# A GELU network's first product: y and its weights in two scaled fp16 parts each, three products of parts in place of float32 ones

## What is computed

```python
def _L1_attn_ref(x, wq, wk, wv, w1, b1, w2, b2, g1, be1, g2, be2):   # D_MODEL = 256, D_FF = 1024
    ...                                    # linear attention: msg
    x = x + msg
    x2 = _layernorm(x, g2, be2)            # the kernel's y
    h = jax.nn.gelu(x2 @ w1.T + b1, approximate=False)
    x = x + (h @ w2.T + b2)
    return x
...
x = L0_attn_inputs
x = x + _layernorm(_L0_attn_ref(_layernorm(x), ...))
x = x + _layernorm(_L0_ffn_ref(_layernorm(x), ...))
x = x + _layernorm(_L1_attn_ref(_layernorm(x), ...))
x = x + _layernorm(_L1_ffn_ref(_layernorm(x), ...))
```

## Time and profile before

| | |
|---|---|
| Timed executions | 3266.88, 3273.56, 3274.42 us, median 3273.56 |
| Profiled execution | 3264.48 us, of which 3262.7 us is the span from its first to its last instruction |
| Mean granted TensorE clock | 0.979 of 2.4 GHz |
| Softmax attention | from 0 to about 2047 us |
| Later layers | from about 2047 us to the end |
| Busy in the span | TensorE matmul 90%, ScalarE 71%, VectorE 46%, GpSimd 7% |
| Memory traffic | 54 GB/s on average |

### The profile page before, as it was taken

How to read it: one execution, slowest core, us unless ns; L and a number is a source line. 1 busy time by engine, 2 the same in 40 slices (tenths; PEclk the granted TensorE clock), 3 DMA queues, 4 the chain that set the end, 5 groups by cost and what they waited for, 6 DMA issues and landing times. The chain is left out here.

```text
span 3262.7 us, 47962 instructions
## 1 busy us (share of the span) xinstructions
PE 2933.2 (90%) x18048; PEld 1175.9 (36%) x18048; DVE 1487.4 (46%) x3540; ACT 2324.9 (71%) x2581; POOL 217.2 (7%) x193
## 2 busy tenths in 40 slices
PE   0899998999999999999999999389999999999986
PEld 0121221222222222222222222156666666666654
DVE  7231130322432333223420311558888888866674
ACT  0999999999999999999999999223333333433332
POOL 0000000000000000000000000011111111111110
PEclk9999999999999999999999999689999999999998
DMA  3310110310210221111110110212111211111010
GB/s 121 117 51 27 54 54 25 92 53 25 80 54 24 80 80 34 50 54 50 61 53 25 48 35 26 66 46 79 57 59 58 81 60 58 45 46 59 26 46 21
DMA packets 124714, 177.69 MB, mean 54 GB/s; under 512 B 41936, under 2 KB 99536, under 8 KB 124240
## 3 DMA queue, kind: packets, MB, share of 16 engines
q1 hardware_dynamic: 124496, 174.76, 16.6%
HBM read 107.62 MB, written 67.11 MB: 54 GB/s over the span
## 5 line engine op out<-in xcount | busy, mean ns | idle before, releaser
L663 ACT ACTIVATE probs<-ps 128x1024 f32<-128x1024 f32 x2048 | 1894.8, 1172 | 49.2 <-PE ps L436 48.0
L562 PE MATMUL ps<-probs,vals 128*32 128x512 f32 x8192 | 1097.8, 609 | 0.0
L436 PE MATMUL ps<-qT,kT 64*128 64x512 f16 x4096 | 731.2, 387 | 109.9 <-DMA kT<-split_dram 27.9
L436 PEld LDWEIGHTS ps<-qT,kT 64*128 64x128 f16 x4096 | 173.7, 93 | 1151.2 <-ACT probs L663 1026.6
L811 DVE COPY sums<-ps 128x512 f32<-128x512 f32 x64 | 44.3, 692 | 527.6 <-PE ps L562 527.6
L562 PEld LDWEIGHTS ps<-probs,vals 128*32 128x32 f32 x8192 | 163.0, 108 | 297.6 <-issue 234.0
L1235 PE MATMUL layers_ps<-yT,weight_mem 128*128 128x512 f32 x512 | 227.5, 595 | 10.9 <-ACT hT L1474 10.9
L1241 PE MATMUL layers_ps<-weight_mem,hT 128*128 128x256 f32 x1024 | 231.5, 380 | 0.0
L1501 ACT ACTIVATE gate<-layers_ps 128x512 f32<-128x512 f32 x96 | 57.3, 597 | 224.4 <-PE layers_ps L1389 224.4
L1241 PEld LDWEIGHTS layers_ps<-weight_mem,hT 128*128 128x128 f32 x1024 | 193.5, 190 | 29.4
L1389 PE MATMUL layers_ps<-n4T,weight_mem 128*128 128x512 f16 x768 | 177.0, 385 | 7.3 <-DVE n4T L1724 7.3
(11 more groups left out here) (223 smaller groups left out, 2614.9 us busy)
## 6 DMA issues: line engine op xcount, KB each, us to landing
split_dram<-parts SPq DMA_DIRECT2D x28, 768.0 KB, 3.7
qT<-split_dram SPq DMA_DIRECT2D x128, 128.0 KB
kT<-split_dram SPq DMA_DIRECT2D x128, 128.0 KB
xs<-in_x_dram SPq DMA_DIRECT2D x4, 2048.0 KB, 13.2
qT<-split_dram SPq DMA_DIRECT2D x128, 64.0 KB
kT<-split_dram SPq DMA_DIRECT2D x128, 64.0 KB
heads_dram<-result SPq DMA_DIRECT2D x64, 128.0 KB, 7.5
q_in<-q_dram SPq DMA_DIRECT2D x16, 512.0 KB, 3.3
```

The costliest lines, as they stand in the source:

```text
L436: last = nc.tensor.matmul(SCORES[slot][:, n * BANK:(n + 1) * BANK], kT[buf][rows, j * P:(j + 1) * P], qT[buf][rows, q0:q0 + BANK], start=T ...
L562: mm = nc.tensor.matmul(ACC[32 * c:32 * c + 32, :], vals[buf][:, j, :], probs[:, j % PROBS, c * BANK:(c + 1) * BANK], start=(j == 0), stop ...
L663: nc.scalar.activation(probs[:, j % PROBS, half * T // 2:(half + 1) * T // 2], SCORES[slot_of(at)], ACT.Exp, scale=OPERAND_SCALE ** -2).th ...
```

## The change

The float32 products of `fc0` and `fc1` are replaced by fp16 ones. y and `w1` are each multiplied by a scale and split into a high and a low fp16 part. For each block of 128 hidden channels TensorE makes three products of parts (high w1 with high y, low w1 with high y, high w1 with low y), each over two halves of the 256 channels: six fp16 matmuls of 512 columns in place of two float32 ones. GELU gets the inverse scale as a per-partition operand.

ScalarE now writes the high part (with the scale) and raises `yT_high`; a new VectorE stage `y_low` makes the low part from PSUM and raises `yT_done`. `y_low` stands behind `k_feat` in the list of `all` and between `o` and `diag` in that of `drain`. In the softmax program VectorE finds the largest `w1` at head 57, makes the scales at head 58 (nine small instructions) and splits `w1` in place at head 59 (three instructions over 2048 columns).

```diff
-STAGES = {... "m": "msg y yT",
+STAGES = {... "m": "msg y yT y_low",
...
-    "all": "ffn x4 b2 mix out n4 in0 n4_low f up0 up1 low0 low1 x2 up2 up3 low2 low3 msg n2 up4 up5 low4 low5 u y k_low o k_feat in1 q_low in2 q_feat kv diag".split(),
-    "drain": "x4 b2 ffn n4 out n4_low up0 up1 low0 low1 up2 up3 low2 low3 msg up4 up5 low4 low5 y o diag".split()}
+    "all": "ffn x4 b2 mix out n4 in0 n4_low f up0 up1 low0 low1 x2 up2 up3 low2 low3 msg n2 up4 up5 low4 low5 u y k_low o k_feat y_low in1 q_low in2 q_feat kv diag".split(),
+    "drain": "x4 b2 ffn n4 out n4_low up0 up1 low0 low1 up2 up3 low2 low3 msg up4 up5 low4 low5 y o y_low diag".split()}
...
@@ TensorE, fc
-                        chan_out(ps[:, 6 + i % 2, :], W["w1"], i, yT).then_inc(sem("fc_mm"), 1)
+                        for n, (s, t) in enumerate(((0, 0), (1, 0), (0, 1))):
+                            for k in range(KC):
+                                last = nc.tensor.matmul(ps[:, 6 + i % 2, :], w1_16[:, s, k, i * P:(i + 1) * P], yT16[:, t, k, :],
+                                                        start=(n == k == 0), stop=(n == 2 and k == KC - 1))
+                        last.then_inc(sem("fc_mm"), 1)
@@ ScalarE
-                A(yT[:, :, :], banks(0, 2), ACT.Copy).then_inc(sem("yT_done"), 1)
+                A(yT16[:, 0, :, :], banks(0, 2), ACT.Copy, scale=y_scale).then_inc(sem("yT_high"), 1)
...
-                        A(hT[:, i, :], ps[:, 6 + i % 2, :], ACT.Gelu, bias=W["b1"][:, 0, i:i + 1]).then_inc(sem("gelu_done"), 1)
+                        A(hT[:, i, :], ps[:, 6 + i % 2, :], ACT.Gelu, scale=fc_back, bias=W["b1"][:, 0, i:i + 1]).then_inc(sem("gelu_done"), 1)
@@ VectorE
+            def y_low(c, past):
+                dve.wait_ge(sem("yT_high"), c + 1)
+                V.scalar_tensor_tensor(yT16[:, 1, :, :].rearrange("p a n -> p (a n)"), wide(0, 2), y_scale, yT16[:, 0, :, :].rearrange("p a n -> p (a n)"),
+                                       ALU.mult, ALU.subtract).then_inc(sem("yT_done"), 1)
@@ VectorE, softmax program, heads 57 to 59
+                    V.tensor_reduce(widest_weight[:, 1:2], flat(W["w1"]), AX.X, ALU.max, apply_absolute_value=True).then_inc(weights_ready, 1)
...
+            def parts_of_w1():
+                ...
+                ch.link(V.tensor_scalar(scaled, w1, fc_scale[:, 1:2], None, ALU.mult))
+                ch.link(V.tensor_copy(high, scaled))
+                ch.link(V.tensor_tensor(low, scaled, high, ALU.subtract))
```

More of the change, by code:

```diff
@@ L68 @@
 NORM_SCALE, HIDDEN_SCALE = 2048.0, 0.5
+W1_MAX, Y_MAX = 2.0 ** 12, 2.0 ** 14
+ROOT_C = C ** 0.5
 FLOAT_WEIGHTS = (("wr", KC, C), ("wk", KC, C), ("wv", KC, C), ("aq", KC, C), ("akv", KC, 2 * C), ("w1", KC, F1), ("w2", M1, C),
@@ new lines, in first_half, with scales_of_w1 @@
+                    scales_of_w1()
+                if last_group and e == 3:
+                    parts_of_w1()
+            def scales_of_w1():
+                ch = Chain(dve, weights_ready, 3)
+                tmp = lambda i: fc_scale[:, i:i + 1]
+                ch.done(V.tensor_scalar(tmp(4), widest_weight[:, 3:4], TINY, None, ALU.max))
+                ch.done(V.tensor_reduce(tmp(5), W["g2"], AX.X, ALU.max, apply_absolute_value=True))
+                ch.link(V.tensor_reduce(tmp(6), W["be2"], AX.X, ALU.max, apply_absolute_value=True))
+                ch.link(V.scalar_tensor_tensor(tmp(3), tmp(5), ROOT_C, tmp(6), ALU.mult, ALU.add))
+                ch.link(V.tensor_scalar(tmp(3), tmp(3), TINY, None, ALU.max))
+                ch.link(V.reciprocal(fc_scale[:, 0:2], fc_scale[:, 3:5]))
+                ch.done(V.tensor_scalar(tmp(0), tmp(0), Y_MAX, None, ALU.mult))
+                ch.done(V.tensor_scalar(tmp(1), tmp(1), W1_MAX, None, ALU.mult))
+                ch.link(V.scalar_tensor_tensor(tmp(2), tmp(3), 1 / (Y_MAX * W1_MAX), tmp(4), ALU.mult, ALU.mult))
+                assert ch.n == W1_SCALED - 3
@@ L985, in second_half @@
+            def parts_of_w1():
+                ch = Chain(dve, weights_ready, W1_SCALED)
+                scaled, w1 = flat(xs[:, 0:KC * F1 // C, :]), flat(W["w1"])
+                high, low = (w1.bitcast(FP16)[:, s * KC * F1:(s + 1) * KC * F1] for s in range(2))
+                ch.link(V.tensor_scalar(scaled, w1, fc_scale[:, 1:2], None, ALU.mult))
+                ch.link(V.tensor_copy(high, scaled))
+                ch.link(V.tensor_tensor(low, scaled, high, ALU.subtract))
             def second_half(head, general):
@@ L1022, in _ @@
             second_half(NHD - 1, False)
-            dve.wait_ge(weights_ready, 3)
+            dve.wait_ge(weights_ready, W1_SCALED + 3)
 SHIFT = {"0": -EARLY, "1": 1 - EARLY, "2": 2 - EARLY, "l": LEAD, "m": LEAD + 1, "a": LEAD + 2, "b": LEAD + 3, "c": LEAD + 4}
 FIRST_CHUNK = {stream: EARLY if stream in "012" else 0 for stream in SHIFT}
-STAGES = {"0": "load_in in0 in1 in2 keep_x1", "1": "mix mix_r mix_k val f x2 n2 u", "2": "uT k k_low k_feat v q q_low q_feat kv", "l": "load_msg diag", "m": "msg y yT",
+STAGES = {"0": "load_in in0 in1 in2 keep_x1", "1": "mix mix_r mix_k val f x2 n2 u", "2": "uT k k_low k_feat v q q_low q_feat kv", "l": "load_msg diag", "m": "msg y yT y_low",
           "a": "load_x2 b2 fc0 fc1 proj0 proj1 proj2 proj3 o",
@@ L1100, in run, with later_layers @@
                 once(it, first, streams)
-def later_layers(nc, heads_in, x_in, W, W16, int_weights, narrow, ident, x2_dram, n2_dram, q_dram, kv_sums, sem, out):
+def later_layers(nc, heads_in, x_in, W, W16, int_weights, narrow, ident, x2_dram, n2_dram, q_dram, kv_sums, fc_scale, sem, out):
     with ExitStack() as ctx:
@@ L1761, in program @@
                 stages = {"in0": in0, "in1": in1, "in2": in2, "mix": mix, "f": f_layer, "x2": x2_layer, "n2": n2_layer, "u": u_layer,
-                          "k_low": k_low, "k_feat": k_features, "q_low": q_low, "q_feat": q_features, "kv": kv, "diag": diag, "msg": msg, "y": y_in,
+                          "k_low": k_low, "k_feat": k_features, "q_low": q_low, "q_feat": q_features, "kv": kv, "diag": diag, "msg": msg, "y": y_in, "y_low": y_low,
                           "o": o_layer, "x4": x4_layer, "n4": n4_layer, "ffn": ffn_stats(exact16), "out": finish,
```

19 lines of the change are left out of this document (12 added, 7 removed).

## The result

The changed kernel takes 3300.05 us (median of four, 3298.27 to 3300.99); the kernel before, run beside it, 3273.99 (3266.88 to 3274.49). The ratio is 1.0079, with a 95% interval of 1.0067 to 1.0092: 26 us slower. The profiled execution took 3300.85 us, with a span of 3299.0 us and a mean granted clock of 0.966, where before had 3262.7 and 0.979.

A forecast was written before the change was run, and what follows sets the result against it. Bound: TensorE from `mix_k` to `k`, then VectorE from `k_low` to `mix`. Order +5.1 and clock +15.5 make +20.6 us on 3264.48, giving 3285; taken as 3290 towards the timed median, range 3268 to 3307.

The forecast's parts named there:

- the order: VectorE's chain in iterations 5 to 12: `y_low`, taken as 1.23 us, is paid eight times, +9.8 us.
- The products: `fc` blocks on TensorE: 0.43 us less a block, 55 us for 128 blocks, bringing nothing in iterations 5 to 12.
- The rival that TensorE counts: Waits before `mix_k` come from TensorE's own lateness, so 55 us less work shows in full: 3210 us; chance 8%.
- The clock at `mix_k`: Waits of 4.6 us before every `mix_k` lower TensorE's clock: +9.5 us (bounds 0 and +13).
- The wait before `q`: TensorE waits 2.3 us for `yT_done`; clock lost in about half the cases, +6 including drain waits (bounds 0 and +9).
- Iterations 12 to 14: `q` comes 2.3 to 2.6 us later with nothing queued on VectorE to cover it: +3.1 us of order.
- The drain: Iterations 15 to 18: TensorE's savings against `y_low` give -7.8 us of order; clock at waits before `up0` costs +2.
- Softmax program: Preparing `w1` on VectorE at three heads falls into its idle time: 0 us (bounds 0 and +5).
- The partial rival: VectorE's slow `xk` loses its collision, 2 us in 8 iterations, with little clock loss: -10 to -30; chance 4%.
- the rival with an unchanged clock: Order costs +5.1 us, `mix_k` slows no more often than now: 3270 (3279 against the median); chance 22%.

The follow-up runs named there:

- `y_low` alone: The kernel before with float32 products kept and only a VectorE instruction of `y_low`'s form added, raising `yT_done`: 3287.80 us, ratio 1.0049.
- `y_low` twice: The changed kernel with the `y_low` instruction issued twice in a row: 3320.28 us.
- The filled wait: The changed kernel with 14 unused fp16 matmuls put on TensorE before its wait ahead of `mix_k`: 3282.83 us, ratio 1.0033.
- the products alone: The changed kernel without `y_low`, the third product using the high part of y once more: 3272.84 us, ratio 1.0002.
- the moved addition and the fill: The changed kernel with GpSimd's `o = x3 + b2` moved behind `in0` and seven filling matmuls before `mix_k`: 3269.42 us, ratio 0.9986.
- Taking the wait away: The changed kernel with moved addition and seven filling matmuls, plus `y_low` before `k_feat` and `down3` before `q`: 3258.81 us, ratio 0.9958.
- the third reordering: The changed kernel with `mix` and `out` before `x4`, `val`, `proj0`, `proj1` earlier, `y_low` before `k_feat`, `down3` before `q`: 3291.31 us, ratio 1.0060.

## Why the prediction was right, and where it was not

Forecast were 3290 us and slower, with a range of 3268 to 3307; measured were 3300. The mechanism was right: VectorE's chain ends last, `y_low` is paid in it, the saved products are not, and the longer wait costs clock. The size was not. The sum was +20.6 us against the profiled execution of before (span 3262.7), and there the loss is 36.3 us. That 3300 lies in the range is in part luck: that execution was a low one, the forecast was moved up by 5 us for it, and the upper end of 3307 is reached by the terms that it names only with the 5 us of the softmax program added (3274.42 + 5.1 + 13 + 9 = 3301.5). The 36.3 us lie as follows.

**Periods.** The `mix_k` of iterations 4 and 12 start 621.1 us apart after and 596.5 before: +24.6 in eight periods. The lengths of `mix_k` in between hold 15.6 us of lost clock more than before; the other 9.0 are order. 9.8 had been forecast for the order (`y_low`, taken as 1.23 and measured at 1.27, eight times). `y_low` alone showed the term (75.5 us a period instead of 74.4); `y_low` twice added another 13.4, clock included.

**The products.** Forecast was that their 55 us do not show in the periods and give some in the drain. The run with the cheap products and no `y_low` gave no difference that can be measured: its trace has 11.9 us more in the periods, for the clock, and 4.6 less behind them, and the rest is within the spread of the kernel before. The rival that TensorE counts, as the Trainium skill has it (Perfetto Trace Analysis, Identifying the Most-Contended Engine: optimize the engine with the highest occupancy first), fell here: TensorE, the busiest at 90%, was relieved and nothing came of it; an addition on GpSimd, at 7%, that slowed VectorE, at 46%, held the 22 us (16 to 18 of them in the periods).

**The clock at `mix_k`: the mis-sized term.** Forecast were 8 x 1.6 - 2 x 1.7 = 9.5 us, with a bound of 13. Measured are 20.5 us in the eight `mix_k` after and 3.4 before: 17. The step that failed is the price of one spell. It was taken from a row behind 2 us of idle time (5.39 us instead of 3.70), for waits that would be 4.6 us long. They were: 4.45 to 4.52 in five of eight. But behind them `mix_k` took up to 6.64 us, 2.94 more than at full clock, and the sum over the eight lies outside the bound. The filled wait gave back 17 us, the same number from the other side. No single price would have been right either: behind waits of 4.3 to 4.9 us a `mix_k` lost between 1.4 and 3.0 us in the runs with the products alone and with `y_low` twice, and why one lost more than another is open. With the measured 17 us in place of 9.5 the sum would have been 3292 against the profiled execution, and the forecast near 3297.

**The wait before `q`.** Forecast 2.3 us, measured 2.3 to 2.4, and hidden in the iterations 5 to 11 of the change. There it took no clock from any `q`, where about half had been forecast. In other runs it did: four of the eight `q` with the filled wait, five of the eight with the moved addition and the fill. There `q_low` came late by up to 0.99 us and the period was 1 us longer. Taking the wait away gave 2.2 us in the periods and 6.2 behind them.

**Iterations 12 to 14.** From `mix_k` of iteration 12 to `up0` of iteration 14: +9.1 us. Forecast were 3.1 for the order, 1.6 for the clock of `mix_k` and 2 for that of the two `q`. `mix_k` lost 1.57, each `q` 1.7, and the `up0` of iteration 13 took 6.27 us where it took 5.31 before: 5.9 of clock, which leaves 3.2 for the order, as forecast.

**The drain.** From `up0` of iteration 14 on the kernel gained 3.3 us; forecast were 7.8, less 2 for the clock. `up0` waits 1.9 us for `n4_low` in iteration 16, as expected, and between the `up0` of 15 and 16 and of 16 and 17 the change is 1.2 and 2.1 us shorter, where 1.3 and 2.1 were forecast. Around them clock was lost: the `up0` of iteration 14 took 5.30 us instead of 3.61, and `down1` to `down3` 5.53 us in iteration 14 and 5.45 in 17 instead of 4.09. From `up0` of 14 to that of 15 the change is 0.7 us longer, from 17 to 18 only 0.7 shorter, where 1.3 and 3.1 less were forecast.

**Softmax program.** Forecast 0. The part ended at 2050.5 us after and 2046.3 before, but in the other twelve profiled runs at 2046.2 to 2052.1, the kernel before run again at 2052.1 and `y_low` twice, which prepares `w1`, at 2046.2: it varies by itself. The 4.1 us were there at head 57, before `w1` is first touched, and did not grow behind it. The rest, 1.7 us up to the `mix_k` of the fourth iteration, is not explained by a run.

**The partial rival.** At 4% it was noted that `xk` takes 3.39 us where 1.4 is usual, and might lose its collision by chance. It did not, since GpSimd's list moves with VectorE's. But to name a collision and not ask who collides, and whether that one could be elsewhere, was the largest omission: it was worth as much as the whole loss.

**Rows misread.** "Three of four waits near 2 us were harmless" is wrong: of the five of 1.94 to 2.00 us two lost clock, as the same text says in another place, so the rival with an unchanged clock had less for it. Not every idle time above 2.5 us took the clock either: behind one of 3.70 us, at 2156.64, eight transposes ran at a granted clock of 1.00. The waits of 2.43 to 2.45 us in the drain that were free in that trace took the clock in the second trace of the same kernel (12 fp16 matmuls in 2.63 to 2.72 us instead of 1.47). And 55 us less than the median of 3273.56 are 3219, not 3215.

Left open is why the third reordering stood at 78.4 us a period; its waits (2.17 us before `nT`, 1.53 before `msg`, 2.95 for the first GELUs) are in the trace, but no run took them apart.

## What to carry to other kernels

Read which engine's work ends last at the wait that closes the loop, and price an edit by which side of that wait it is on. Work taken from the other side only makes the wait longer, and a longer wait has a price of its own on TensorE's clock. Take that price from waits of the same length, and as a range: behind waits of 4.3 to 4.9 us it was 1.4 to 3.0 us here. Where two halves of a change are measured alone, compare the periods and not only the totals: the totals hid that the cheaper products cost 12 us in the loop. When two rows of the same form on an engine differ by a factor, look what GpSimd does in that microsecond before planning a reordering of stages: moving one addition that nobody waits for did what three reorderings and a cheaper product did not.

## What the runs showed of the hardware

- Behind idle times of TensorE of 4.45 to 4.52 us, eight float32 records that take 3.70 us took 6.53 to 6.64 in the change; behind 4.57 to 4.88 us in the run with the products alone 5.12 to 6.53; behind 2.51 us 5.39; behind 2.38 us 3.67 in one iteration and 5.37 in another of the same run. The length of the idle time alone does not tell the loss. The view of stretches gives a granted clock of 0.50 (1.2 GHz) inside such a spell. Matmuls whose result nobody reads, put into the wait, kept the clock at its upper level and gained 17 us.
- An addition on GpSimd with both inputs in SBUF (2.55 us) makes two VectorE instructions with two SBUF inputs take 3.38 us instead of 1.41: moved away, they took 1.41 or 1.42 in four runs, and where it had nothing to stand behind, in iteration 12, 3.39. Four instructions with one SBUF tile as input took 3.33 us beside it instead of 1.38, in a run that did not isolate it. An instruction that reads PSUM and one SBUF tile was not touched (1.23 us beside it). The Trainium skill (SBUF — State Buffer, Who interferes with whom) has the pair of ports that the two engines share as an exclusive lock for which the second to come waits; by that rule the loss should be near the 2.16 us left of the addition when `xk` starts, and the traces agree with 1.98.
- ScalarE's GELU with its scale from memory takes 0.78 us where it took 0.69. It is hidden behind the 1.30 us of a block.
